# Graph attention with LayerNorm: the main loop in half quads, comparisons of 1024 columns, converting adjacency transfers

## What is computed

```python
Wh = (h @ W.T).reshape(n, K, OUT_DIM).transpose(1, 0, 2)
e = jax.nn.leaky_relu(score_src + score_dst, NEG_SLOPE)
e = jnp.where((adj == 0)[None, :, :], -jnp.inf, e)
alpha = jax.nn.softmax(e, axis=-1)
h_prime = jnp.einsum('kij,kjd->kid', alpha, Wh)
return h_prime.transpose(1, 0, 2).reshape(n, K * OUT_DIM)
...
x = _layernorm(x + _L0_gnn_ref(x, adj, L0_gnn_W, L0_gnn_a), axis=-1)
```

## Time and profile before

| | us |
|---|---|
| median of three runs | 1604.79 |
| the profiled execution | 1607.59 |
| its span in the profile | 1605.8 |
| up to the main loop | about 88 |
| after the last quad | about 23 |

### The profile page before, as it was taken

One profiled execution on the slowest core, in us unless ns is written; L12 is line 12 of the kernel. 1 busy time (PEld: TensorE's weight loads), 2 busy tenths in 40 slices (PEclk: granted clock), 3 DMA queues, 4 the chain that ended last, 5 costly groups with the idle time before them and its releaser, 6 DMA issues.

```text
span 1605.8 us, 77792 instructions
## 1 busy us (share of the span) xinstructions
PE 1205.8 (75%) x35205; PEld 1166.5 (73%) x35205; DVE 1544.2 (96%) x2158; ACT 1488.6 (93%) x1834; POOL 1368.7 (85%) x1473
## 2 busy tenths in 40 slices
PE   6047778777777887787878777778778778787884
PEld 6046777777776877787777777768777777777884
DVE  7978999999999999999999999999999999999995
ACT  3799999999899999999999999999999999999883
POOL 1847898989888889898989899888889889998995
PEclk9579999999999999999999999999999999999998
DMA  4425565666665566656657565665666566565650
GB/s 162 134 88 180 166 215 184 216 198 204 196 202 190 186 215 198 206 193 206 219 173 231 195 201 188 202 205 187 206 205 204 185 213 222 171 222 172 203 182 23
DMA packets 162564, 303.01 MB, mean 189 GB/s; under 512 B 10296, under 2 KB 22968, under 8 KB 162232
## 3 DMA queue, kind: packets, MB, share of 16 engines
q1 hardware_dynamic: 162232, 298.03, 57.2%
HBM read 293.67 MB, written 4.33 MB: 186 GB/s over the span
## 4 chain that ended last, share of the span: by engine, by line
ACT 50%; DVE 20%; PE 16%; issue 7%; POOL 1%; POOLq 0%; DVEq 0%; ACTq 0%
ACT kept L467 37%; PE bank L781 14%; ACT step L467 10%; DVE rest L665 5%; DVE rest L663 4%; DVE step L636 4%; DVE kept L655 4%; PE bank L768 2%; ACT late L494 2%; DVE step L650 1%; ACT y L500 1%; DVE step L648 1%; DVE stats L691 0%; DVE step L653 0%; POOL late L365 0%
## 5 line engine op out<-in xcount | busy, mean ns | idle before, releaser
L467 ACT ACTIVATE kept<-s_two,sd 128x1024 uint8<-128x1024 f32 (+1 forms) x1024 | 1065.8, 1119 | 54.2 <-PE bank L781 51.9
L417 POOL TENSOR_SCALAR step<-s_own,sd 128x512 uint8<-128x512 f32 x1040 | 710.5, 702 | 13.5 <-PE bank L781 12.0
L781 PE MATMUL bank<-F,rest 128*128 128x66 f16 x16384 | 549.3, 193 | 38.5 <-issue 37.4
L351 POOL TENSOR_SCALAR edge<-adj_t 128x2048 int8<-128x2048 int32 x256 | 484.8, 1894 | 94.7 <-PE bank L768 74.8
L781 PEld LDWEIGHTS bank<-F,rest 128*128 128x128 fp8e4 x16384 | 528.0, 98 | 39.7 <-issue 38.3
L781 PE MATMUL bank<-G,kept 128*128 128x66 f16 x8192 | 422.6, 194 | 47.1 <-issue 35.7
L781 PE MATMUL bank<-G,step 128*128 128x66 f16 x8192 | 423.4, 193 | 33.6 <-issue 33.2
L636 DVE SCALAR_TENSOR_TENSOR step<-s_own,sd,bank 128x512 uint8<-128x512 f32 x496 | 347.6, 742 | 15.1 <-PE bank L768 14.9
L781 PEld LDWEIGHTS bank<-G,kept 128*128 128x128 fp8e4 x8192 | 320.9, 98 | 55.9 <-issue 39.7
L781 PEld LDWEIGHTS bank<-G,step 128*128 128x128 fp8e4 x8192 | 320.8, 97 | 39.7 <-issue 39.7
L467 ACT ACTIVATE step<-s_own,sd 128x512 uint8<-128x512 f32 x512 | 340.6, 718 | 0.0
(11 more groups left out here) (83 smaller groups left out, 518.7 us busy)
## 6 DMA issues: line engine op xcount, KB each, us to landing
adj_t<-in_adj SPq DMA_DIRECT2D x512, 512.0 KB, 4.8
s_own<-sT_scratch SPq DMA_DIRECT2D x32, 256.0 KB, 5.9
s_two<-sT_scratch SPq DMA_DIRECT2D x31, 256.0 KB, 5.1
kept<-in_x SPq DMA_DIRECT2D x16, 256.0 KB, 5.8
y<-in_x SPq DMA_DIRECT2D x16, 256.0 KB, 5.8
out<-y SPq DMA_DIRECT2D x16, 256.0 KB, 5.2
y<-sT_scratch SPq DMA_DIRECT2D x1, 256.0 KB, 3.7
sT_scratch<-late SPq DMA_DIRECT2D x2, 64.0 KB, 1.9
```

The costliest lines, as they stand in the source:

```text
L351: nc.gpsimd.tensor_scalar(edge[:, k % N8], adj_t[:, k % NA], 1.0, -1.0, ALU.min, ALU.max).then_inc(edge_set, 1)
L417: last = nc.gpsimd.tensor_scalar(step_u8[:, k % NS, h - KEPT, n // E, :, n % E], s_own[:, g % 2, h - KEPT], STEEP, d_steep[:, q * IB + n, ...
L467: return nc.scalar.activation(out, scores, ACT.Sigmoid, scale=STEEP, bias=d_steep[:, q * IB + b, h:h + 1])
L781: last = nc.tensor.matmul(acc[k][:, col:col + width], matrices[h][:, n // E, b * P:(b + 1) * P, n % E], values[:, q * IB + n, h].rearrange ...
```

## The change

The unit of the loop becomes a pair: 2 blocks of 128 columns j (half a quad), 512 units in all, with 32 pairs a group.
- `adj` is loaded by transfers that GpSimd issues and that convert int32 to int8 on the way, 2048 columns wide (8 pairs, `CP`) in two transfers of 256 rows, two chunks deep. `take_edges`, `adj_t` and SyncE's `load_adj` are gone.
- All four heads are treated as heads 0/1 were: in two rings (heads 0/1, heads 2/3), each comparison covers this group and the next, 1024 columns. A pair has 4 of them; ScalarE makes 2 (3 in one pair of 8), GpSimd the others. VectorE makes none. In group 0, 128 first comparisons of 512 columns come on top instead of 64: 30 by GpSimd and 9 by ScalarE before the loop, 3 a pair in it.
- A pair is masked by one `tensor_tensor` and of 1024 words, and its rest taken by one xor of 1024 words, without the constant of ones. VectorE's order is `take_step(k)`, `take_rest(k - 1)`.
- Three PSUM banks take transposed edges; the sums of `G` and of `F` lie apart, in five banks. TensorE adds `step` of pair t, transposes pair t + 2, and adds `rest` of pair t - 1.
- ScalarE and GpSimd wait for `step_done` and `rest_set` of the unit 5 before (`NS`). SyncE loads a group's scores in two transfers of 512 KB in place of four of 256 KB, this group's rows ahead of the next one's. The closing steps move to pairs 2 to 30.

```diff
-    NA = 2
-    N8 = 2
-    NS = 3
-    KEPT = 2
-    PLACES = QUADS + NS
+    CP = 8
+    NC = 2
+    CHUNK = CP * E * P
+    RINGS = HEADS // 2
...
+    PLACES = PAIRS + NS
...
+    NT = 3
+    AHEAD = 2
+    WORDS = ROWS * E // 4
...
+    def tiles(t):
+        n_act = 3 if t % 8 == 5 else 2
+        every = [(e, r) for r in range(RINGS) for e in range(E)]
+        return every[:n_act], every[n_act:]
...
+    early_pool = FIRST[:30]
+    early_act = {m: FIRST[30 + n] for n, m in enumerate(range(EARLY, UNITS, 2))}
+    rest_first = FIRST[len(early_pool) + len(early_act):]
+    PER_PAIR = -(-len(rest_first) // (PAIRS - 1))
...
+        s_two = sb("s_two", [P, 2, RINGS, 2, ROWS], fp32)
+        edge = sb("edge", [P, NC, IB, CHUNK], i8)
+        kept = sb("kept", [P, RINGS, PLACES + NS, WORDS], i32)
+        rest = sb("rest", [P, NL, RINGS, 2, WORDS], i32)
...
+        acc, pre, tr = bank[0:BANKS], bank[0:2 * NU], bank[2 * NU:8]
+        edge_bank = [bank[6], bank[7], bank[5]]
...
+        edgeT16 = [t[:, 0:WORDS].bitcast(bf16) for t in edge_bank]
+        edgeT = [t[:, 0:WORDS].bitcast(i32).unsqueeze(1).unsqueeze(1).to_broadcast([P, RINGS, 2, WORDS]) for t in edge_bank]
...
+            def load_two(g, r):
+                n = min(2, GROUPS - g)
+                to = s_two[:, g % 2, r, 0:n].rearrange("p g i -> p (g i)")
+                sync.dma_start(to, sT[2 * r + g % 2, g * ROWS:(g + n) * ROWS].unsqueeze(0).to_broadcast([P, n * ROWS])
+                               ).then_inc(two_loaded[g % 2], 16)
...
-                    if q in S_QUADS and g + 1 < GROUPS:
+                    if t in S_PAIRS and g + 1 < GROUPS:
...
+                            sync.wait_ge(G1_set, UNITS)
+                        sync.wait_ge(rest_done, pair_no(g, 0) + 1)
+                        load_two(g + 1, S_PAIRS.index(t))
...
-            def take_edges(k):
-                pool.wait_ge(adj_loaded[k % NA], 16 * U * (k // NA + 1))
-                if k >= N8:
-                    pool.wait_ge(transposed, k - N8 + 1)
-                nc.gpsimd.tensor_scalar(edge[:, k % N8], adj_t[:, k % NA], 1.0, -1.0, ALU.min, ALU.max).then_inc(edge_set, 1)
+            def load_edges(c):
+                if c >= NC:
+                    pool.wait_ge(transposed, (c - NC + 1) * CP)
+                for u in range(U):
+                    nc.gpsimd.dma_start(edge[:, c % NC, u * E:(u + 1) * E], adj_v[c // (PAIRS // CP), c % (PAIRS // CP), :, u]
+                                        ).then_inc(edge_loaded[c % NC], 16)
...
+            def compare(out, scores, j, h):
+                return nc.gpsimd.tensor_scalar(out, scores, STEEP, d_steep[:, j, h:h + 1], ALU.mult, ALU.add)
...
+            for c in range(NC):
+                load_edges(c)
...
+            pool.wait_ge(d_set, 1)
+            pool.wait_ge(first_loaded, 32)
+            for tile in early_pool:
+                compare_first(*tile)
...
             for g in range(GROUPS):
-                pool.wait_ge(own_loaded[g % 2], 32 * (g // 2 + 1))
-                for q in range(QUADS):
-                    k = quad_no(g, q)
+                h = g % 2
+                pool.wait_ge(two_loaded[h], 32 * (g // 2 + 1))
+                for t in range(PAIRS):
+                    k = pair_no(g, t)
                     if k >= NS:
-                        pool.wait_ge(rest_done, k - NS + 1)
-                    for n, h in tiles(g, q)[1]:
-                        last = nc.gpsimd.tensor_scalar(step_u8[:, k % NS, h - KEPT, n // E, :, n % E], s_own[:, g % 2, h - KEPT],
-                                                       STEEP, d_steep[:, q * IB + n, h:h + 1], ALU.mult, ALU.add)
+                        pool.wait_ge(step_done, k - NS + 1)
+                        pool.wait_ge(rest_set, k - NS + 1)
+                    if g == 0:
+                        for tile in first_tiles(t)[1]:
+                            compare_first(*tile)
+                    for e, r in tiles(t)[1]:
+                        if g + 1 < GROUPS:
+                            two, in_order = both(k, k + PAIRS)
+                            last = compare(kept_u8[:, r, two, :, e], s_two[:, h, r, ::-1] if in_order else s_two[:, h, r], t * E + e, 2 * r + h)
+                        else:
+                            last = compare(kept_u8[:, r, places(k)[1], :, e], s_two[:, h, r, 0], t * E + e, 2 * r + h)
                     last.then_inc(pool_compared, 1)
-                    if k + N8 < GROUPS * QUADS:
-                        take_edges(k + N8)
-                    if q in CLOSING and g > 0:
-                        close(g - 1, CLOSING.index(q))
-                    if q == 13 and g > 0:
+                    if t % CP == 0 and NC <= k // CP + 1 < GROUPS * PAIRS // CP:
+                        load_edges(k // CP + 1)
+                    if t in CLOSING and g > 0:
+                        close(g - 1, CLOSING.index(t))
+                    if t == DEVIATION and g > 0:
...
-                    for b in range(IB):
+                        act.wait_ge(step_done, k - NS + 1)
+                        act.wait_ge(rest_set, k - NS + 1)
...
+                            two, in_order = both(k, k + PAIRS)
+                            last = compare(kept_u8[:, r, two, :, e], s_two[:, h, r, ::-1] if in_order else s_two[:, h, r], t * E + e, 2 * r + h)
...
+            def take_step(k):
                 dve.wait_ge(transposed, k + 1)
...
-                dve.wait_ge(dve_compared, k + 1)
                 dve.wait_ge(act_compared, k + 1)
                 dve.wait_ge(pool_compared, k + 1)
...
-                nc.vector.scalar_tensor_tensor(kept[:, both(k, k)[0]], edgeT[q % 2], ONES, kept[:, both(k, k)[0]],
-                                               ALU.bitwise_and, ALU.bitwise_and).then_inc(step_set, 1)
-            def take_rest(g, q):
-                k = quad_no(g, q)
+                nc.vector.tensor_tensor(kept[:, :, both(k, k)[0]], edgeT[k % NT], kept[:, :, both(k, k)[0]], ALU.bitwise_and
+                                        ).then_inc(step_set, 1)
+            def take_rest(k):
                 dve.wait_ge(step_set, k + 1)
                 if k >= NL:
                     dve.wait_ge(rest_done, k - NL + 1)
-                nc.vector.scalar_tensor_tensor(rest[:, k % NL, KEPT:HEADS], step[:, k % NS], ONES, edgeT[q % 2],
-                                               ALU.bitwise_xor, ALU.bitwise_and)
-                nc.vector.scalar_tensor_tensor(rest[:, k % NL, 0:KEPT], kept[:, both(k, k)[0]], ONES, edgeT[q % 2],
-                                               ALU.bitwise_xor, ALU.bitwise_and).then_inc(rest_set, 1)
+                nc.vector.tensor_tensor(rest[:, k % NL], kept[:, :, both(k, k)[0]], edgeT[k % NT], ALU.bitwise_xor
+                                        ).then_inc(rest_set, 1)
...
+                for t in range(PAIRS):
+                    take_step(pair_no(g, t))
+                    if t > 0:
+                        take_rest(pair_no(g, t - 1))
+                    if t >= FINISH and t % 2 == 0:
                         next(closing, None)
+                take_rest(pair_no(g, PAIRS - 1))
...
+            def transpose_edges(k):
+                c = k // CP
+                if k % CP == 0:
+                    pe.wait_ge(edge_loaded[c % NC], 16 * U * (c // NC + 1))
+                if k >= NT:
+                    pe.wait_ge(rest_set, k - NT + 1)
+                for b in range(IB):
+                    last = nc.tensor.transpose(edgeT16[k % NT][:, b * P:(b + 1) * P],
+                                               edge16[:, c % NC, b, k % CP * P:(k % CP + 1) * P], identb[:, :])
                 last.then_inc(transposed, 1)
...
+            def add_step(g, t):
+                k = pair_no(g, t)
+                pe.wait_ge(step_set, k + 1)
...
+            def add_rest(g, t):
+                k = pair_no(g, t)
+                add_pair(t, [rest_f8[:, k % NL, r, side] for r, _, side in by_head(g, k)], F, CHUNKS,
...
+                for t in range(PAIRS):
+                    k = pair_no(g, t)
+                    add_step(g, t)
+                    if t > 0:
+                        pe.wait_ge(rest_set, k)
+                    if k + AHEAD < GROUPS * PAIRS:
+                        transpose_edges(k + AHEAD)
+                    if t > 0:
+                        add_rest(g, t - 1)
+                pe.wait_ge(rest_set, pair_no(g, PAIRS - 1) + 1)
+                add_rest(g, PAIRS - 1)
```

More of the change, by code:

```diff
@@ L31, in gat_layernorm @@
     TINY = 1e-37
-    ONES = 0x01010101
     U, E = 2, 2
@@ L184, in gat_layernorm @@
         s_stored = sem("s_stored")
-        own_loaded = [sem(f"own_loaded{n}") for n in range(2)]
-        two_loaded = [sem(f"two_loaded{n}") for n in range(KEPT)]
+        two_loaded = [sem(f"two_loaded{n}") for n in range(2)]
         first_loaded = sem("first_loaded")
@@ L198, in gat_layernorm @@
         f_set = sem("f_set")
-        adj_loaded = [sem(f"adj_loaded{n}") for n in range(NA)]
```

(28 more changed lines are left out.)

265 lines of the change are left out of this document (76 added, 189 removed).

## The result

The changed kernel takes 1538.61 us, the median of four runs (1537.06 to 1542.16), against 1604.13 before on the same chip (1601.57 to 1605.15): a ratio of 0.9597, 95% interval 0.9576 to 0.9617, 4.0% less time. The profiled execution took 1542.16 us, its span is 1540.4. The forecast was 1450, 9.6% less.

A forecast was written before the change was run, and what follows sets the result against it. The bound moves from VectorE to GpSimd: 88 before the loop + 107 for group 0 + 14 x 82.7 + 75 + 23 = 1451 us of span, median 1450, 9.6% less than 1604.8; range 1340 to 1640.

The forecast's parts named there:

- The last group and the end: Last terms of the sum: 75 us for the last group, set by VectorE, and 23 us for the end.
- GpSimd's 1.07: Main loop: a GpSimd comparison of 1024 columns costs 1.07 us, 60 of them 64.2 us a group.
- The issue: Main loop: each transfer issued by GpSimd costs it 1.0 us, bounds 0 and 1.9; 8 us a group.
- groups 1 to 14: Main loop: GpSimd's comparisons 64.2, closing work 10.5 and issues 8 make 82.7 us a group.
- the 0.67 line: Main loop: GpSimd's 512-column comparison stays at the loop's 0.67 us, not the 1.10 seen while `weigh` ran.
- more work gives no row a reason to lower it: TensorE in the loop: its clock, 1.00 while it is 79% busy, stays there.
- about 75: TensorE in the loop: 2.3 us a pair, 74 a group, about 75 with ten small bank openings and closings.
- the start: Before the loop: ScalarE arrives at 88 us, +5 as bound; `x` in by about 29, last block used about 35.
- (a): Rival: GpSimd's issues nearly free or overlapped, all four engines meet at 75 us a group; 1343 to 1357; chance 0.14.
- (b): Rival: GpSimd dearer, comparisons of 1.34 us or issues of 1.9; 1678 or 1552 us; chance 0.16, half slower.
- (c): Rival: converting transfers at half rate or less, transposes wait for loads; about 1840 us; chance 0.15, 0.11 slower.
- (d): Rival: coupling with five pairs of lead costs 0.3 us a pair; 92 a group, 1580 us; chance 0.04.

The follow-up runs named there:

- both disturbances removed: Changed kernel with `shift` moved to GpSimd and `adj` transfers after the first two chunks cut to 64 of 2048 columns: 1467.51 us, ratio 0.9164.
- the run with the later issue: `adj` loads issued one pair later, against the kernel with `shift` on GpSimd, `x` first and 72/56 comparisons: 1480.15 us, ratio 0.9236 against 0.9151.
- thin loads: Changed kernel with each `adj` transfer after the first two chunks carrying 64 of 2048 columns, same issues and rows: 1527.43 us, ratio 0.9538.
- the run without loads: Changed kernel with no chunk of `adj` loaded after the first two, GpSimd's issues gone too: 1391.33 us in one run.

## Why the prediction was right and wrong

**Right: direction, bound and prices.** VectorE, 96% busy before, is relieved; GpSimd becomes the busiest. VectorE's `tensor_tensor` takes 1.21 us, ScalarE's comparison 1.14, as the forecast took them. The last group and the end took 97.5 where 98 stood, but that is luck: 79.5 for 75, and an end of 18.0 for 23. GpSimd's 1.07 was 1.10: here the estimate by the Trainium skill, GPSIMD Engine Reference, section 3.1, 1.11, was the closer one. The issue was 0.745 where I chose 1.0. The two errors cancel by luck, and with both disturbances removed the mean is 82.6 for 82.7. The median lies inside the stated range, 1340 to 1640, and the gain is 4.0% where 9.6% was forecast.

**Wrong in size: groups 1 to 14, 87.66 for 82.7.** I gave the bound engine's sum as the group, while VectorE, at 74.7, and TensorE, at 75, had 8 us of slack that I took to cover everything. Two steps failed.

The first is "the new and and xor read one operand from PSUM, so the 0.67 line holds". It was right for those, and I had read the contention in the earlier trace rows, 1.10 against 0.67 while `weigh` ran. What I did not do is go through the other VectorE instructions of the loop for two operands in SBUF. `shift` is one, and cost 174 ns before: in 13 of groups 1 to 14 it began in the last 0.15 us of a GpSimd instruction, and once 0.44 us before its end, and took 443 ns. With the change GpSimd has 60 comparisons of 1.1 us and little else, and `shift` stands through five of them. It is worth 3.3 to 4.4 us a group.

The second is "more work gives no row a reason to lower it", of TensorE's clock, and with it "about 75" for TensorE. The waits view of before has 106.2 us of gaps marked "issue" on TensorE, 6 or 7 us a group, and I left them out since they had cost nothing there. With 75 + 6.6, my estimate from these rows, TensorE is at about 82, at the new bound and not 8 below it, and the matmuls behind a gap or a hole are slower. The runs bear it out: 99.4% of the loop is TensorE's work and its gaps once GpSimd has less to do. The loads are worth 0.7 to 1.8 us a group.

**Wrong: the start, 14 us for at most 5.** "`x` in turns with them by about 29, while its last block is used about 35" reckoned with the total. But the blocks are used one after the other, each waits for its own landing, and `x` shared the engines with the converting transfers. The window from 8 to 20 us, changed kernel above, kernel before below:

```profile
8.00:20.00 12.00, 5.60 (x24) 5.19 (x25) 1.58 (x6) 1.34 (x3) 0.00 (x0) 1.00 1.07 138
```

```profile
8.00:20.00 12.00, 11.59 (x90) 11.51 (x90) 9.12 (x37) 4.22 (x9) 0.00 (x0) 1.00 1.09 361
```

The DMA engines are full in both, and 138 GB/s arrive in place of 361 (a converting transfer counts by the bytes that it writes, 67.12 MB on the page for all of `adj`, so a part is counting), while TensorE, on `x`, is busy half as long. Moving the loads behind `x` returned 17.8 us at the first matmul.

**Small:** the sum has no wait of GpSimd at its issues; it waits 57.8 us there for TensorE. In the run with the later issue 39.6 us less of it gained nothing.

**The rivals.** (a), issues free, isn't the case: 745 ns each. (b) had the direction of the comparisons, which are 3% dearer and not 25%; the issues are cheaper. (c) fell: a chunk lands in 12.3 us and is wanted 18 to 23 us later; DMA releases none of TensorE's transposes in the loop. The estimate for it by the Trainium skill, DMA: Bandwidth & Descriptors, section Anatomy of one DMA, 13.6, was near. (d) is the nearest in the time that it gives, but its mechanism, five pairs of lead being too few throughout, is shown only with a lead of three.

**Open.** Why an instruction packet comes late while `adj` is loaded: the bytes matter (thin loads, with as many issues, end it), rows of half the length in twice as many transfers do not help, and I have no run on the rest. Why `shift` stands through five comparisons here, and through one in the run without loads and in the kernel before. How the hole's 3.3 to 4.4 us divide into the wait and the slow matmuls behind it: no run holds the clock. Six smaller slots for transposed edges in three PSUM banks, which would give TensorE more lead over VectorE, were not tried.

## What to carry to other kernels

When a change moves the bound, read the waits of each engine that comes near to it, the rows marked "issue" too: a wait that costs nothing before is a term of the sum after. Before giving GpSimd a long unbroken run of work, look on VectorE for every small instruction between its big ones, those with two operands in SBUF first; move it, or let GpSimd wait for it once (0.9336 and 0.9307 here, for 0.9597). A bulk load put at the front of a kernel shares the DMA engines with the small loads that the first compute waits for.

## What was not expected of the hardware

- A VectorE instruction of 4 columns with two SBUF operands was held 5.37 us, until the fifth of five GpSimd comparisons in a row ended, in twelve of fourteen groups; in the run without loads the same instruction was let go after one comparison, with the next already begun. With GpSimd pausing, it took 151 ns. A small instruction with one SBUF operand (L671) took 170 ns wherever no comparison of GpSimd ran beside it (all groups of the run without loads) and 2131 with a lead of three, where one did; how long it is held stays unexplained.
- A converting transfer of 256 rows, issued by GpSimd, occupies it for 741 to 750 ns on average, whether it carries 64, 1024 or 2048 columns. Two together, 4.2 MB of int32, land in 12.3 us.
- TensorE has gaps of up to 3.0 us that no engine ends, behind packets of its own instructions: 84 to 111 in a kernel of 35173 matmuls when `adj` is loaded in full (40 with a lead of three), and 7 to 11 when it isn't.
